# Third and fourth tile behind the layer turned by DMA instead of TensorE, in a fused scan and expert kernel

## The reference, cut to what matters

```
def _L0_attn_ref(x, A, ...):                 # x is the layer-normalised input
    s  = sigmoid(silu(x @ s_w1.T + s_b1) @ s_w2.T + s_b2)
    u  = (x @ B_w.T + B_b) * s
    h_t = h_{t-1} @ A.T + u_t                # scan over 4096 tokens, 128 states
    y  = h @ C_w.T + C_b + x @ D_w.T + D_b
    return y * sigmoid(x @ g_w.T + g_b)
def _L0_ffn_ref(x, gate_w, expert_w):        # x is layer-normalised again
    chosen = argmax(x @ gate_w.T)            # one of 8 experts for each token
    return x + x @ expert_w[chosen].T
x = x + attn(layernorm(x));  x = x + ffn(layernorm(x))
```

## Time and profile before

| what | value |
|---|---|
| median of three runs | 936.96 us |
| the profiled execution, its own time | 938.51 us |
| its span | 936.8 us |
| TensorE matmul busy | 915.0 us, 98% |
| VectorE busy | 683.1 us, 73% |
| ScalarE busy | 617.6 us, 66% |
| GpSimd busy | 388.0 us, 41% |
| mean granted TensorE clock | 0.994 |

### The profile page before, as it was taken

One profiled execution on the slowest core, in us unless ns is written; L12 is line 12 of the kernel. 1 busy time (PEld: TensorE's weight loads), 2 busy tenths in 40 slices (PEclk: granted clock), 3 DMA queues, 4 the chain that ended last, 5 costly groups with the idle time before them and its releaser, 6 DMA issues. The chain is left out here.

```text
span 936.8 us, 15953 instructions
## 1 busy us (share of the span) xinstructions
PE 915.0 (98%) x4657; PEld 749.4 (80%) x4658; DVE 683.1 (73%) x1670; ACT 617.6 (66%) x874; POOL 388.0 (41%) x508
## 2 busy tenths in 40 slices
PE   8999999999999999999999999999998999999995
PEld 7777888888888888888888888888776878888884
DVE  6787979888897978889797888877875554444442
ACT  5568686867768586776768676776355656665661
POOL 1032627173553618164462717355242453333332
PEclk9999999999999999999999999999999999999998
DMA  8436484655648574665748385564989676555430
GB/s 315 121 90 146 95 212 106 186 142 152 160 111 204 112 203 115 170 144 136 192 98 213 100 187 140 153 163 141 338 305 385 228 262 208 159 163 166 139 116 36
DMA packets 179304, 159.51 MB, mean 170 GB/s; under 512 B 103957, under 2 KB 137493, under 8 KB 178208
## 3 DMA queue, kind: packets, MB, share of 16 engines
q1 hardware_dynamic: 168288, 124.86, 50.0%
q0 software_dynamic: 10800, 33.70, 10.2%
q10 hardware_dynamic: 144, 0.07, 0.0%
HBM read 81.63 MB, written 54.68 MB: 146 GB/s over the span
## 5 line engine op out<-in xcount | busy, mean ns | idle before, releaser
L1556 PE MATMUL y<-experts,x1T_hi 128*128 x568 | 183.9, 405 | 2.0 <-issue 1.3
L539 POOL TENSOR_SCALAR ln_var_eps<-ln_mean_var 128x4 f32<-128x4 f32 x16 | 3.6, 224 | 301.3 <-DVE ln_mean_var L951 301.2
L586 POOL DMA_INDIRECT out<-gate,ids x71 | 70.2, 989 | 137.0 <-DVE gate L1251 86.4
L1556 PEld LDWEIGHTS y<-experts,x1T_hi 128*128 128x128 f32 x568 | 102.2, 190 | 21.4 <-issue 3.1
L1251 DVE TENSOR_TENSOR gate<-y,raw_weights 128x512 f32<-128x512 f32 x71 | 49.1, 692 | 91.5 <-PE y L1556 91.2
L1556 PE MATMUL y<-experts,x1T_lo 128*128 x284 | 112.3, 395 | 0.0
L1276 PE MATMUL gates<-GwT_hi,xT_hi 128*128 128x512 f32 x256 | 104.6, 409 | 0.0
L694 ACT ACTIVATE joined<-flipped 128x1024 uint16<-128x1024 uint16 x60 | 82.3, 1372 | 32.7 <-DVE xT_lo L1094 23.2
L1276 PE MATMUL y<-DwT_hi,xT_hi 128*128 128x512 f32 x256 | 101.9, 398 | 0.5 <-DVE gateT L873 0.5
L1277 PE MATMUL y<-DwT_lo,xT_hi 128*128 128x512 f32 x256 | 100.4, 392 | 0.0
L1278 PE MATMUL y<-DwT_hi,xT_lo 128*128 128x512 f32 x256 | 100.3, 392 | 0.0
(11 more groups left out here) (272 smaller groups left out, 2324.5 us busy)
## 6 DMA issues: line engine op xcount, KB each, us to landing
raw_weights<-routed_rows SPq DMA_DIRECT2D x71, 258.0 KB, 2.7
x_in<-L_attn_x SPq DMA_DIRECT2D x32, 512.0 KB, 4.9
x_rows<-L_attn_x SPq DMA_DIRECT2D x32, 512.0 KB, 4.9
turned_experts<-raw_weights SPq DMA_DIRECT2D x32, 512.0 KB, 4.6
experts<-turned_experts SPq DMA_DIRECT2D x8, 2048.0 KB, 11.8
raw_weights<-L_ffn_expert_w SPq DMA_DIRECT2D x32, 256.0 KB, 3.0
routed_rows<-padrow SPq DMA_DIRECT2D x9, 258.0 KB
out<-gate,ids POOLq DMA_INDIRECT x71, 2.8
```

The costliest lines, as they stand in the source:

```text
L586: nc.gpsimd.indirect_dma_start(out=out_rows, out_offset=bass.IndirectOffsetOnAxis(ap=ids[r][:, 0:1], axis=0), in_=res[r], in_offset=None, ...
L1556: ins = nc.tensor.matmul(Y[m % 2][:], x2T[a][:, k, m % 2 * P:(m % 2 + 1) * P], flat[:, bass.ds(first + (w * KD + k) * D, D)], start=(k == ...
```

## The change

Tiles 2 and 3 of the tail are no longer turned by TensorE, for the tails of blocks 0 to 13 (bodies 1 to 14). ScalarE writes each x1 tile as two planes (`halve_x1`), SyncE issues a DMA transpose for each, ahead of the flips of the next block, ScalarE joins the turned planes (`join_x1`), and `tail_hi` and `tail_lo` read the joined tile in SBUF. The planes and joined tiles lie in `yb`, whose rows are used up by then. The tail of block 14, in the last body, is turned as before.

Three orders change with it. On TensorE, the eight router products of the first pair stand alone after `to_chunks` and after `over` 0; `over` 3 and `gates(b, 1, 2, 3)` trade places, so that `over` 4 follows the gates directly; the second pair's router products move from before `over` 4 to behind `over` 5, and the second `tail_back` from before `over` 5 to behind `down`. On VectorE, `ln2_stats` of the fourth tile moves from behind `place` to behind `over` 0, `tail_lo` of tile 2 from behind `over` 0 to behind `over` 2, that of tile 3 from behind `over` 2 to behind `over` 4, and `low_piece` from there to behind `place`. On ScalarE, the gate of the last tile moves behind the first sigmoid of the next body, the second `scoresT` ahead of the second `join`, and `join(b+1, 2)` behind the copy of the states.

```diff
+        def by_dma(b, i):
+            return b < LASTB - 1 and i >= NT // 2
+        x1_halves = [yb[:, j, :].bitcast(u16) for j in range(2)]
+        x1_flipped = [yb[:, 2 + j, :].bitcast(u16).rearrange("p (c t) -> p c t", t=P) for j in range(2)]
+        x1_joined = [yb[:, j, :] for j in range(2)]
...
 (SyncE, ahead of the flips of the next block)
+                if b > 0 and not last:
+                    for j in range(2):
+                        sp.wait_ge(S_["x1_halves"], 2 * (b - 1) + j + 1)
+                        sp.dma_start_transpose(x1_flipped[j], x1_halves[j]).then_inc(x1_turned[j], 16)
...
 (ScalarE)
+            def halve_x1(b, i):
+                act.wait_ge(S_["x1_ready"], NT * b + i + 1)
+                nc.scalar.activation(x1_halves[i - 2]..., planes(xrow[b % 2][:, i, 0:D]), ACT.Copy)
+            def join_x1(b, i):
+                act.wait_ge(x1_turned[i - 2], 16 * (b + 1))
+                nc.scalar.activation(planes(x1_joined[i - 2]), x1_flipped[i - 2]..., ACT.Copy)
...
-                    gates(b - 1, NT - 1)
...
+                    if tail and m == 0:
+                        gates(b - 1, NT - 1)
...
+                if tail and ahead:
+                    halve_x1(b - 1, 2)
+                    halve_x1(b - 1, 3)
                 if ahead:
                     halve(b + 1, 0)
                     halve(b + 1, 1)
...
+                if tail and ahead:
+                    for i in range(2, NT):
+                        join_x1(b - 1, i)
+                        tail_hi(b - 1, i)
+                    join_piece(b, 0)
...
 (VectorE)
                 over(b, 0)
+                elif tail:
+                    ln2_stats(old, oldq, 3)
...
                 over(b, 2)
+                if tail and ahead:
+                    tail_lo(old, 2)
...
                 over(b, 4)
                 if tail and ahead:
-                    low_piece(b, 0)
+                    tail_lo(old, 3)
...
 (TensorE, bodies 1 to 14)
+                    over(b, 3)
+                    gates(b, 1, 2, 3)
+                    over(b, 4)
+                    y_dense(b, 3, 0, 1)
+                    over(b, 5)
+                    tail_scores(b - 1, 1)
+                    gates(b, 2, 0)
+                    to_middles(b)
+                    gates(b, 2, 1, 2, 3)
+                    y_dense(b, 3, 2)
+                    down(b)
+                    y_dense(b, 3, 3)
+                    tail_back(b - 1, 1)
```

More of the change, by code:

```diff
@@ L191, in preln_ssm_moe_kernel @@
                      "rank_psum pos_ready picked_ready run_ready dest_ready ids_ready ends_ready pad_sent "
-                     "experts_in table_step slot_iota_made expert_table need_table row_table "
+                     "x1_halves x1_joined experts_in table_step slot_iota_made expert_table need_table row_table "
                      "slot_norm slot_turned slot_hi slot_lo slot_psum slot_base slot_ids slot_result").split():
@@ L199, in preln_ssm_moe_kernel @@
         x_turned = [sem("x_turned_even"), sem("x_turned_odd")]
+        x1_turned = [sem("x1_turned_third"), sem("x1_turned_fourth")]
         xres_loaded = [sem("xres_loaded_even"), sem("xres_loaded_odd")]
@@ L307, in turn_bank, with on_pe @@
             return ((SA, G) if b == LASTB else (TP, Y[NT - 1]))[i % 2]
+        def by_dma(b, i):
+            return b < LASTB - 1 and i >= NT // 2
+        def on_pe(b, i):
+            return NT // 2 * min(b, LASTB - 1) + NT * max(0, b - LASTB + 1) + i + 1
+        x1_halves = [yb[:, j, :].bitcast(u16) for j in range(2)]
+        x1_flipped = [yb[:, 2 + j, :].bitcast(u16).rearrange("p (c t) -> p c t", t=P) for j in range(2)]
+        x1_joined = [yb[:, j, :] for j in range(2)]
         def score_bank(b):
@@ L640, in tail_hi @@
             def tail_hi(b, i):
-                act.wait_ge(S_["x2T_psum"], NT * b + i + 1)
-                nc.scalar.activation(turned_rows(b, i)[0][:, :, i % 2 * P:(i % 2 + 1) * P], by_block(turn_bank(b, i)), ACT.Copy
-                                     ).then_inc(S_["x2T_hi"], 1)
+                if by_dma(b, i):
+                    act.wait_ge(S_["x1_joined"], 2 * b + i - 1)
+                    src = x1_joined[i - 2].rearrange("p (k t) -> p k t", k=KD)
+                else:
+                    act.wait_ge(S_["x2T_psum"], on_pe(b, i))
+                    src = by_block(turn_bank(b, i))
+                nc.scalar.activation(turned_rows(b, i)[0][:, :, i % 2 * P:(i % 2 + 1) * P], src, ACT.Copy
+                                     ).then_inc(S_["x2T_hi"], 1)
+            def halve_x1(b, i):
+                act.wait_ge(S_["x1_ready"], NT * b + i + 1)
+                nc.scalar.activation(x1_halves[i - 2].rearrange("p (h d) -> p h d", h=2), planes(xrow[b % 2][:, i, 0:D]), ACT.Copy
+                                     ).then_inc(S_["x1_halves"], 1)
+            def join_x1(b, i):
+                act.wait_ge(x1_turned[i - 2], 16 * (b + 1))
+                nc.scalar.activation(planes(x1_joined[i - 2]), x1_flipped[i - 2].rearrange("p (h k) t -> p h (k t)", h=2), ACT.Copy
+                                     ).then_inc(S_["x1_joined"], 1)
             def scoresT(b, pair):
@@ L750, in body @@
                     join_piece(b, 1)
-                if tail:
                     tail_hi(b - 1, 2)
                     tail_hi(b - 1, 3)
+                if tail:
                     scoresT(b - 1, 0)
-                    if ahead:
-                        join_piece(b, 0)
+                if tail and ahead:
[3 more added lines that the diff above has]
+                    join_piece(b, 0)
                 if ahead:
@@ L762, in body @@
                     halve(b + 1, 2)
+                    if tail:
+                        scoresT(b - 1, 1)
                     join(b + 1, 1)
-                if tail:
+                if b == LASTB:
                     scoresT(b - 1, 1)
@@ L769, in body @@
                     halve(b + 1, 3)
-                    join(b + 1, 2)
+                    if not tail:
+                        join(b + 1, 2)
                 act.wait_ge(S_["scan_lo"], NSTEP * (b + 1))
@@ L956, in tail_lo @@
                 hi, lo = [h[:, :, i % 2 * P:(i % 2 + 1) * P] for h in turned_rows(b, i)]
-                nc.vector.tensor_tensor(lo, by_block(turn_bank(b, i)), hi.bitcast(f32), ALU.subtract
+                src = x1_joined[i - 2].rearrange("p (k t) -> p k t", k=KD) if by_dma(b, i) else by_block(turn_bank(b, i))
+                nc.vector.tensor_tensor(lo, src, hi.bitcast(f32), ALU.subtract
                                         ).then_inc(S_["x2T_lo"], 1)
@@ L1148, in body @@
                 over(b, 0)
-                if tail:
+                if not ahead:
                     tail_lo(old, 2)
+                elif tail:
+                    ln2_stats(old, oldq, 3)
                 over(b, 1)
@@ L1186, in body @@
                     place(old, oldq, oldturn)
-                    ln2_stats(old, oldq, 3)
+                    if ahead:
+                        low_piece(b, 0)
+                    else:
+                        ln2_stats(old, oldq, 3)
                 if ahead:
@@ L1338, in y_dense @@
                     if i == NT - 1:
-                        wait(pe, S_["x2T_lo"], NT * b)
+                        wait(pe, S_["x2T_lo"], NT * b if b == LASTB else NT * (b - 1) + 2)
                 dense(Y[i], i, DwT, ks, False)
@@ L1497, in body @@
                 to_chunks(b)
-                if tail:
+                if b == LASTB:
                     tail_turn(b - 1, 1 - q, 2, True)
+                elif tail:
+                    for n in range(KD):
+                        score_product(b - 1, 0, n)
                 gates(b, 0, 1, 2)
                 over(b, 0)
-                if tail:
+                if b == LASTB:
                     tail_turn(b - 1, 1 - q, 3, True)
+                elif tail:
+                    for n in range(KD, 2 * KD):
+                        score_product(b - 1, 0, n)
                 gates(b, 0, 3)
@@ L1511, in body @@
                     tail_back(b - 1, 0)
[L1512 to L1515, removed]
-                    tail_scores(b - 1, 1)
-                over(b, 4)
-                y_dense(b, 3, 0, 1)
-                if tail:
-                    tail_back(b - 1, 1)
[L1521 to L1527, removed]
+                if not tail or b == LASTB:
+                    gates(b, 1, 2)
+                    over(b, 3)
+                    gates(b, 1, 3)
+                    if tail:
+                        tail_scores(b - 1, 1)
+                    over(b, 4)
+                    y_dense(b, 3, 0, 1)
+                    if tail:
+                        tail_back(b - 1, 1)
+                    over(b, 5)
+                    gates(b, 2, 0, 1)
+                    to_middles(b)
+                    gates(b, 2, 2, 3)
+                    y_dense(b, 3, 2)
+                    down(b)
+                    y_dense(b, 3, 3)
+                else:
+                    over(b, 3)
```

(12 more changed lines are left out.)

## The result

The changed kernel takes 938.56 us (median of 20 runs), the one before 936.84 us in the same comparison: ratio 1.0015, 95% interval 1.0008 to 1.0022. The forecast was 937.8. So 12.5 us of transposes left TensorE, and the kernel became 1.4 to 1.7 us slower. The changed kernel's profiled execution took 937.96 us, with a span of 936.1.

What follows compares the result with a forecast made beforehand. TensorE's order was taken as the bound in the blocks. 13 settled bodies gaining 0.17 us each (2.2) against 3.0 lost in block 1 gave 0.8 us slower: 937.8 us against the median of 936.96, range 930 to 944.

Steps and rivals of the forecast that it cites:

- What leaves TensorE: Transposes removed from TensorE, priced by distances between matmul starts: 0.89 us a body, 12.5 us in 14 bodies, the ceiling.
- the holds: TensorE waiting for VectorE at `over` 5 and the second router products, 0.37 us each in a settled body.
- What the order gives back: The new order holds TensorE for VectorE, 0.74 us a body, leaving a settled body 0.17 us net gain.
- X: The start of the last matmul of `gates(b, 1)`, from which the prediction timed TensorE and VectorE.
- ScalarE: Planes and joins add 4.9 us a body; slack before the hidden layer shrinks from 1.45 to 0.7 us, costing nothing.
- The queue: On SyncE's queue, two more transposes of some 1.9 us each push the next block's landings by up to 3.7 us.
- Block 1: The first x1 transpose queues behind two 512 KB stores, so the hidden layer starts 3.0 us later, once.
- The sum: Over the whole kernel, 13 settled bodies gain 2.2 us and block 1 costs 3.0: 0.8 us slower.
- The first rival: VectorE does not hold TensorE, the transposes' time comes out whole, less block 1's 3.0: 9.5 us, 927.5; chance 0.2.
- The second: ScalarE's chain before the hidden layer becomes the bound: 9.5 us slower, 946.5 us; chance 0.25.

Runs made afterwards that it cites:

- e3: The changed kernel with one more k of `y_dense(b, 3)` moved from behind the gate products to ahead of `over` 5: 930.27 us, ratio to before 0.9925.
- e9: e4 with two gate products instead of one between `over` 5 and `to_middles`: 932.87 us, ratio to before 0.9947.
- e10: e9 and e2 together: 925.93 us, ratio to before 0.9882.
- e1: The changed kernel, but body 1 has its old orders and turns its tail on TensorE: 937.34 us, ratio to before 0.9999.
- e6: e3 and e2 together: 928.87 us, ratio to before 0.9912.
- e5: e3 with `gates(b, 2, 0)` ahead of the second pair's router products, putting them 0.68 us later: 939.71 us, ratio to before 1.0023.
- e8b: The changed kernel with one and a half more DMA transposes, to unread tiles, in each of bodies 1 to 14: 978.64 us, ratio to before 1.0433.
- e2: The changed kernel, but in body 1 SyncE issues the two x1 transposes ahead of the two 512 KB stores: 935.87 us, ratio to before 0.9987.
- e4: The changed kernel with low parts of tiles 2 and 3 around `over` 2, second router products between gate products and `over` 4: 940.73 us, ratio to before 1.0034.
- e7: e3 and e1 together: 926.19 us, ratio to before 0.9887.

## Why the prediction was right, step by step

- *What leaves TensorE.* 0.89 us a body was predicted. With the holds filled, bodies fall from 41.62 to 40.82 (e3, e9), so 0.80 is shown. The rest is not lost at the hidden layer, which follows the state product by 2.80 us in e3 as before. In e3 `over` 4 still loses 0.1 us; where e9 and e10 lose it is not shown.
- *What the order gives back.* 0.37 us at `over` 5 and 0.37 at the router products were predicted, none at `over` 4; 0.27, 0.32 and 0.11 were lost, 0.70 instead of 0.74. The walk on VectorE came out to 0.03 us: with X at 299.63, the gate sum starts at X + 0.43 (predicted 0.43), `tail_lo` at X + 2.03 (2.02), `over` 5 at X + 2.17 (2.2) and the router products at X + 2.77 (2.8). What was missed is the small hold at `over` 4, which was called level; it took from the hold at `over` 5, so the sum hardly moved. (TensorE's three terms up to `over` 5 add up to 1.81, not 1.83.) The state product started at 311.49 - 285.04 = 26.45 (26.44 predicted), the body lasts 41.49 (41.45 predicted). e3 shows that it was a hold: filling it gave back 0.67 us.
- *ScalarE.* The second `scoresT` at 18.5 (18.6 predicted), the last high part ready at 28.3 (28.5). Its load was 33.91 us a body where 34.7 was predicted, and the slack 0.85 where 0.7 was. That was enough in all settled bodies of this profile, though not in those of e1 and e6; e5 measures it.
- *The queue.* 1.9 us a transpose was estimated, with a start-up that no row gives; the queue's share shows 2.0 for the added ones, their own packets 1.7. The first flip landed 11.5 us, the second 15.4 us into the example body, within the bounds. The 1.0 us that the prediction worked out from the 261 GB/s of the Trainium skill (DMA: Bandwidth & Descriptors, latency and other measured facts) is not what these transposes cost here. But e8b shows that I judged the queue's room too large: my walk let it absorb up to 3.7 us.
- *Block 1.* 3.0 us predicted, 2.95 measured, at the step that was named: the first x1 join behind the two stores. The copy of the states stood at 102.29 - 0.88 = 101.4 (101.5 predicted). e2 removed it by the queue's order alone.
- *The sum.* 3.0 - 13 x 0.17 gave +0.8 us; measured +1.4 to +1.7. The term that was too large is the settled body's 0.17, which was 0.12 on average (0.7 us over 13 bodies); the sum by measured terms is 2.95 - 1.5 = +1.45.
- The first rival (the whole gain comes out, less body 1's loss) describes e3, where the hold is covered and body 1's loss stays: 7.1 us faster than before by the ratio of medians, where the rival had 9.5. The second (ScalarE the bound) describes e5.

What stays open is why e1, e2, e4, e5, e6 and e9 have late bodies in their profiles and the changed kernel, e3, e7 and e10 none or next to none: each is one execution, and the queue's landings differ from body to body.

## What to carry to other kernels

Work taken off the bounding engine comes out only where its neighbours' answers are ready sooner too: follow the hand-over between the two engines step by step, from the last instruction that both need, and put independent work in the gap that opens. A new transfer costs by its place in the queue, so look separately at each block whose queue differs from the settled one. An engine whose in-order chain has 0.85 us of slack in a block of 41.5 is nearly a second bound, though it is busy for only 82% of the block. And a reordering has to be walked up to the next hand-over behind it: e4 covered two steps and opened the third.

## What was not expected of the hardware

28 added DMA transposes of 256 KB raised the busy time of the 16 DMA engines by 55 us, 2.0 us each. Each transpose moves in 1024 packets of 256 bytes, a size that nothing else in this kernel has. These packets alone take 147 us of 16 engines for 92 transposes before (1.6 us each) and 202 us for 120 after (1.7 us each); the 21 whole transposes' worth that e8b adds bring them to 226 us, 1.2 us each. So a transpose has no single price here, but even the 1.6 us before are more than twice what a plain 256 KB would take at the 340 to 380 GB/s that some stretches of the trace before moved (0.7 to 0.8 us, an estimate). Added next to the scatters of 258 KB, one and a half more lengthened a body by 2.7 us, 1.8 us for each whole one: at that point hardly any of their time was hidden.

TensorE's granted clock fell from 1.00 to 0.50 in body 1 of e4 and e9, around the longest standstills of its matmuls within the blocks: in e9 1.7 us into one of 3.2 us, in e4 0.9 us after one of 3.3 us had ended. It stayed low for 3.4 us in e4 and 6.8 in e9, and TensorE worked through all of it in e4 and 5.3 us of it in e9. In body 1 of the changed kernel the matmuls stood still for 1.5, 0.9 and 0.4 us at three places, and the clock stayed at 1.00.
